# Attention's row sums: eight pair sums of a half folded into one by accumulating DMAs, multiplied with ones two halves later

## The reference, cut to what matters

```
q = (x @ q_w.T).reshape(b, s, 16, 32).transpose(0, 2, 1, 3)
k = x @ k_w.T;  v = x @ v_w.T                       # one head of 32
scores = jnp.einsum('bhqd,bkd->bhqk', q, k) * SCALE
attn = jax.nn.softmax(scores, axis=-1)
out = jnp.einsum('bhqk,bkd->bhqd', attn, v)
```

## Time and profile before

| what | us |
|---|---|
| median of three runs (4967.91 to 4980.27) | 4971.23 |
| profiled execution, its own time | 4975.68 |
| its span | 4974.1 |
| busy in the span: PE / PEld | 4767.6 / 3697.1 |
| busy in the span: DVE / ACT / POOL | 2952.8 / 2256.3 / 2330.5 |

### The profile page before, as it was taken

How to read it: one execution, slowest core, us unless ns; L and a number is a source line. 1 busy time by engine, 2 the same in 40 slices (tenths; PEclk the granted TensorE clock), 3 DMA queues, 4 the chain that set the end, 5 groups by cost and what they waited for, 6 DMA issues and landing times. The chain is left out here.

```text
span 4974.1 us, 92399 instructions
## 1 busy us (share of the span) xinstructions
PE 4767.6 (96%) x32156; PEld 3697.1 (74%) x32157; DVE 2952.8 (59%) x5707; ACT 2256.3 (45%) x4559; POOL 2330.5 (47%) x1775
## 2 busy tenths in 40 slices
PE   6999996999999999999999699999899999999999
PEld 4788884666666666666666478888799987689999
DVE  6222226788888888888883622222655548675444
ACT  4222224366666666666663422222544435454343
POOL 1545424188888888888882154542411107420000
PEclk8999997899999999999999799999999999999999
DMA  7223227544334443343434722322533212251110
GB/s 222 79 88 105 89 76 265 191 81 78 76 76 79 79 80 75 76 80 78 81 67 148 220 82 91 105 86 78 176 102 102 94 62 78 65 195 52 52 52 31
DMA packets 254023, 496.58 MB, mean 100 GB/s; under 512 B 31728, under 2 KB 86000, under 8 KB 253424
## 3 DMA queue, kind: packets, MB, share of 16 engines
q0 software_dynamic: 62656, 220.24, 19.5%
q1 hardware_dynamic: 191024, 271.73, 16.6%
HBM read 262.74 MB, written 121.63 MB: 77 GB/s over the span
## 5 line engine op out<-in xcount | busy, mean ns | idle before, releaser
L1463 DVE TENSOR_REDUCE attend_mx<-attend_am_ps 128x1 f32<-128x512 f32 x2048 | 1247.8, 677 | 197.8 <-PE attend_am_ps L1338 197.7
L1449 POOL TENSOR_TENSOR attend_pairs<-attend_pt 128x1024 f32<-128x1024 f32 x512 | 1219.0, 2421 | 231.8 <-ACT attend_pt L1429 231.5
L1429 ACT ACTIVATE attend_pt<-attend_sc_ps 128x512 f32<-128x512 f32 x2048 | 1053.8, 620 | 307.6 <-PE attend_sc_ps L1326 305.4
L1338 PE MATMUL attend_am_ps<-attention_kst,attend_qst 96*128 96x512 f32 x2048 | 866.0, 427 | 9.0 <-DMA attend_qst<-q_parts 8.9
L1326 PE MATMUL attend_sc_ps<-attend_qst,attention_kst 98*128 98x512 f32 x2048 | 817.2, 400 | 1.3 <-ACT attend_pt L1429 1.1
L1338 PEld LDWEIGHTS attend_am_ps<-attention_kst,attend_qst 96*128 96x128 f32 x2048 | 392.7, 192 | 243.3 <-issue 102.9
L718 DVE TENSOR_TENSOR expert_ac<-expert_gu_ps,expert_gl 128x512 f32<-128x512 f32 x144 | 99.5, 691 | 668.7 <-ACT expert_gl L682 663.8
L1353 PE MATMUL attend_pv_ps<-attend_pt,attention_v 128*32 128x256 f32 x8192 | 491.6, 380 | 0.0
L1326 PEld LDWEIGHTS attend_sc_ps<-attend_qst,attention_kst 98*128 98x128 f32 x2048 | 389.3, 190 | 83.4 <-ACT attend_pt L1429 9.8
L1353 PEld LDWEIGHTS attend_pv_ps<-attend_pt,attention_v 128*32 128x32 f32 x8192 | 259.9, 110 | 188.9 <-issue 23.8
L1817 ACT ACTIVATE ffn_sg<-ffn_gu_ps,ffn_gs 128x256 f32<-128x256 f32 x352 | 166.7, 474 | 508.4 <-PE ffn_gu_ps L1738 508.3
(11 more groups left out here) (348 smaller groups left out, 9310.7 us busy)
## 6 DMA issues: line engine op xcount, KB each, us to landing
attend_pairs<-attend_pairs POOLq DMA_DIRECT2D x192, 512.0 KB
weights_raw<-experts_dram POOLq DMA_DIRECT2D x76, 512.0 KB
ys<-expert_ob SPq DMA_DIRECT2D x144, 256.0 KB
attend_qst<-q_parts SPq DMA_DIRECT2D x192, 128.0 KB, 3.3
yn<-route_yb SPq DMA_DIRECT2D x64, 256.0 KB
ffn_xb<-x SPq DMA_DIRECT2D x64, 256.0 KB, 3.4
ffn_rb<-x SPq DMA_DIRECT2D x64, 256.0 KB
keyvalue_xb<-x SPq DMA_DIRECT2D x64, 256.0 KB, 2.8
```

The lines of the kernel that those rows point to most:

```text
L1338: pe.matmul(am[:, bank, :], qst[0:KROWS, n % 2, h * HALF + hd, :], kst[0:KROWS, o:o + 4 * P], start=True, stop=True).then_inc(am_rdy, 1)
L1429: act.activation(pt[:, u % RING, g * 4 * P:(g + 1) * 4 * P], sc[:, s % SBANKS, :], ACT.Exp, scale=HD ** -0.5).then_inc(p_rdy, 1)
L1449: pool.tensor_tensor(pairs[:, j, :], pt[:, 2 * p % RING, :], pt[:, (2 * p + 1) % RING, :], ALU.add).then_inc(pair_rdy, 1)
L1463: dve.tensor_reduce(mx[:, hh, block:block + 1], am[:, am_slot["max", a] % MBANKS, :], AX.X, ALU.max).then_inc(mx_rdy, 1)
```

## The change

- A half's eight pair sums are folded into one by four DMAs, all accumulating, issued by GpSimd. Fold 0 adds slots of pairs 2, 3 to those of 0, 1 (1 MB, both slots in one DMA), fold 1 adds 4, 5, fold 2 adds 6, 7 (1 MB each), and fold 3 adds the second slot to the first (512 KB). They are issued after GpSimd's pair 4 and 7 of the same half and pair 2 and 5 of the next (FOLD_AFTER = 4, 7, 10, 13), each after a wait for the fold before it.
- TensorE multiplies the one folded slot by ones: one group of four matmuls in a half, at batch 0 two halves later, after a wait for fold 3. The last half isn't folded: its eight pair sums are multiplied one by one at the end.
- The slots of pairs 0 and 1 exist in three sets, the other six once: `pairs` has 12 slots in place of 8. GpSimd's pair 0 of a half waits for the sums three halves back, its pairs 2, 4 and 6 for folds 0, 1 and 2 of the half before.
- The copied values are kept in three sets, the copied sums in two; `keep_sums`, the reciprocals and the output of a half come four batches (one half) later. `raw` (the output weights as loaded) takes the place of the last tiles of `attn`.

```diff
-QUADS = (1, 3, 5)
-LAG_QUAD = 3
-LAG_SUM = 2
+SETS = 3
+FOLD_AFTER = (4, 7, 10, 13)
...
+        def slot(half, j):
+            return 2 * (half % SETS) + j if j < 2 else 2 * SETS + j - 2
...
+            def add_up(half, j, first, last):
                 for i in range(4):
+                    ins = pe.matmul(pv[HD * i:HD * (i + 1), 1, :], const["ones"][:, 0:HD], pairs[:, slot(half, j), 2 * P * i:2 * P * (i + 1)],
+                                    start=first, stop=last, skip_group_check=True)
+                if last:
+                    ins.then_inc(sum_rdy, 1)
+
+            def sums(half):
+                pe.wait_ge(fold_in[-1], 16 * (half + 1))
+                add_up(half, 0, False, True)
...
-                if at == 0 and half:
+                if at == 0 and half >= 1:
                     pe.wait_ge(vals_kept, half)
-                if at == 1 and half:
-                    pe.wait_ge(sums_kept, half)
-                for done, j in batch_sums(c):
-                    sums(done, j)
+                if at == 1 and half >= 2:
+                    pe.wait_ge(sums_kept, half - 1)
+                if at == 0 and half >= 2:
+                    sums(half - 2)
                 for u in range(c * BATCH, (c + 1) * BATCH):
                     values(u)
             pe.wait_ge(vals_kept, HALVES)
-            for done, j in batch_sums(BATCHES):
-                sums(done, j)
+            sums(HALVES - 2)
+            pe.wait_ge(sums_kept, HALVES - 1)
+            for j in range(HPAIRS):
+                pe.wait_ge(pair_rdy, RING // 2 + (HALVES - 1) * HPAIRS + j + 1)
+                add_up(HALVES - 1, j, j == 0, j == HPAIRS - 1)
...
+            def fold(half, k):
+                if not 0 <= half < HALVES - 1:
+                    return
+                to = slot(half, 0)
+                if k:
+                    pool.wait_ge(fold_in[k - 1], 16 * (half + 1))
+                if k < len(FOLD_AFTER) - 1:
+                    pool.wait_ge(pair_rdy, RING // 2 + half * HPAIRS + 2 * k + 4)
+                    put, get = pairs[:, to:to + 2, :], pairs[:, slot(half, 2 * k + 2):slot(half, 2 * k + 2) + 2, :]
+                else:
+                    put, get = pairs[:, to, :], pairs[:, to + 1, :]
+                pool.dma_start(put, get, accum_op=ALU.add).then_inc(fold_in[k], 16)
+
             for p in range(N * PAIRS):
                 half, j = divmod(p, HPAIRS)
-                if half:
-                    pool.wait_ge(sum_rdy, sums_until(half - 1, j))
+                if j == 0 and half >= SETS:
+                    pool.wait_ge(sum_rdy, half - SETS + 1)
+                if j >= 2 and j % 2 == 0 and half:
+                    pool.wait_ge(fold_in[j // 2 - 1], 16 * half)
                 pool.wait_ge(p_rdy, SBANKS + 4 * p + 4)
-                pool.tensor_tensor(pairs[:, j, :], ...).then_inc(pair_rdy, 1)
-                if j in QUADS:
-                    pool.wait_ge(pair_rdy, RING // 2 + p + 1)
-                    pool.dma_start(pairs[:, j - 1, :], pairs[:, j, :], accum_op=ALU.add).then_inc(quad_in[QUADS.index(j)], 16)
+                pool.tensor_tensor(pairs[:, slot(half, j), :], ...).then_inc(pair_rdy, 1)
+                for k, after in enumerate(FOLD_AFTER):
+                    if j == after % HPAIRS:
+                        fold(half - after // HPAIRS, k)
...
-                half, at = divmod(c - PER_HALF - 1, PER_HALF)
+                half, at = divmod(c - 2 * PER_HALF - 1, PER_HALF)
                 if half >= 0:
                     shares(half, at)
                     if at == PIECES - 1:
                         output(half)
```

More of the change, by code:

```diff
@@ L1214, in attention_stage @@
         pt = mem.sb("pt", [P, RING, HALF * P])
-        pairs = mem.sb("pairs", [P, HPAIRS, HALF * P])
+        pairs = mem.sb("pairs", [P, SETS * 2 + HPAIRS - 2, HALF * P])
         mx = mem.sb("mx", [P, HEADS, KBLOCKS])
@@ L1220, in attention_stage @@
         inv = mem.sb("inv", [P, 2 * P])
-        raw = mem.sb("raw", [P, DC, D])
-        kept = mem.sb("kept", [P, 2, 2, 2 * P])
+        vals = mem.sb("vals", [P, SETS, 2 * P])
+        whole = mem.sb("whole", [P, 2, 2 * P])
+        raw = attn[:, NT - DC:NT, :, :].rearrange("p c h q -> p c (h q)")
         sc = mem.ps("sc", [P, SBANKS, 4 * P])
@@ L1227, in attention_stage @@
         m_in = mem.sems("m_in", 2)
-        quad_in = mem.sems("quad_in", len(QUADS))
+        fold_in = mem.sems("fold_in", len(FOLD_AFTER))
         w_in, whi_rdy = mem.sem("w_in"), mem.sem("whi_rdy")
@@ L1240, in attention_stage @@
         PER_HALF = QT // BATCH
-        SUMS = len(QUADS) + HPAIRS - 1 - QUADS[-1]
         AHEAD = 2 * BATCH + SBANKS
@@ L1355, in values @@
                 ins.then_inc(pv_rdy, 1)
-            def sums(half, j):
-                if j in QUADS:
[L1360 to L1364, removed]
-                for i in range(4):
-                    ins = pe.matmul(pv[HD * i:HD * (i + 1), 1, :], const["ones"][:, 0:HD], pairs[:, slot, 2 * P * i:2 * P * (i + 1)],
-                                    start=False, stop=(j == HPAIRS - 1), skip_group_check=True)
-                ins.then_inc(sum_rdy, 1)
+            def add_up(half, j, first, last):
+                for i in range(4):
+                    ins = pe.matmul(pv[HD * i:HD * (i + 1), 1, :], const["ones"][:, 0:HD], pairs[:, slot(half, j), 2 * P * i:2 * P * (i + 1)],
[5 more added lines that the diff above has]
+                add_up(half, 0, False, True)
             for c in range(-LEAD // BATCH, BATCHES):
@@ L1407, in keep_values @@
             def keep_values(half):
-                if half >= 2:
-                    act.wait_ge(o_rdy, half - 1)
+                if half >= SETS:
+                    act.wait_ge(o_rdy, half - SETS + 1)
                 act.wait_ge(pv_rdy, RING + QT * (half + 1))
-                act.activation(kept[:, half % 2, 0, :], pv[:, 0, :], ACT.Copy).then_inc(vals_kept, 1)
+                act.activation(vals[:, half % SETS, :], pv[:, 0, :], ACT.Copy).then_inc(vals_kept, 1)
             def keep_sums(half):
@@ L1417, in keep_sums @@
                     act.wait_ge(inv_rdy, PIECES * (half - 1))
-                act.wait_ge(sum_rdy, SUMS * (half + 1))
-                act.wait_ge(pv_rdy, RING + min(QT * (half + 1) + BATCH, N * UNITS))
-                act.activation(kept[:, half % 2, 1, :], pv[:, 1, :], ACT.Copy).then_inc(sums_kept, 1)
+                act.wait_ge(sum_rdy, half + 1)
+                act.wait_ge(pv_rdy, RING + min(QT * (half + 2) + BATCH, N * UNITS))
+                act.activation(whole[:, half % 2, :], pv[:, 1, :], ACT.Copy).then_inc(sums_kept, 1)
             for s in range(PIECES_ALL):
@@ L1433, in _ @@
                     keep_values(half)
-                if i == 0 and at == 0 and half > 0:
-                    keep_sums(half - 1)
+                if i == 0 and at == 0 and half >= 2:
+                    keep_sums(half - 2)
             keep_values(HALVES - 1)
+            keep_sums(HALVES - 2)
             keep_sums(HALVES - 1)
@@ L1443, in _ @@
                 pool.tensor_tensor(w_lo[:, c, :], raw[:, c, :], w_hi[:, c, :].bitcast(F32), ALU.subtract)
+            def fold(half, k):
[10 more added lines that the diff above has]
+                pool.dma_start(put, get, accum_op=ALU.add).then_inc(fold_in[k], 16)
             for p in range(N * PAIRS):
                 half, j = divmod(p, HPAIRS)
-                if half:
-                    pool.wait_ge(sum_rdy, sums_until(half - 1, j))
+                if j == 0 and half >= SETS:
+                    pool.wait_ge(sum_rdy, half - SETS + 1)
+                if j >= 2 and j % 2 == 0 and half:
+                    pool.wait_ge(fold_in[j // 2 - 1], 16 * half)
                 pool.wait_ge(p_rdy, SBANKS + 4 * p + 4)
-                pool.tensor_tensor(pairs[:, j, :], pt[:, 2 * p % RING, :], pt[:, (2 * p + 1) % RING, :], ALU.add).then_inc(pair_rdy, 1)
-                if j in QUADS:
-                    pool.wait_ge(pair_rdy, RING // 2 + p + 1)
-                    pool.dma_start(pairs[:, j - 1, :], pairs[:, j, :], accum_op=ALU.add).then_inc(quad_in[QUADS.index(j)], 16)
+                pool.tensor_tensor(pairs[:, slot(half, j), :], pt[:, 2 * p % RING, :], pt[:, (2 * p + 1) % RING, :], ALU.add).then_inc(pair_rdy, 1)
+                for k, after in enumerate(FOLD_AFTER):
+                    if j == after % HPAIRS:
+                        fold(half - after // HPAIRS, k)
         @block.vector
@@ L1487, in shares @@
                 cut = slice(2 * P // PIECES * piece, 2 * P // PIECES * (piece + 1))
-                dve.reciprocal(inv[:, cut], kept[:, half % 2, 1, cut]).then_inc(inv_rdy, 1)
+                dve.reciprocal(inv[:, cut], whole[:, half % 2, cut]).then_inc(inv_rdy, 1)
             def output(half):
@@ L1494, in output @@
                 dve.wait_ge(vals_kept, half + 1)
-                dve.tensor_tensor(attn[:, n, h, :], kept[:, h, 0, :], inv[:], ALU.mult).then_inc(o_rdy, 1)
```

(5 more changed lines are left out.)

## The result

The changed kernel takes 5042.1 us (median of four, 5021.6 to 5044.4), the kernel before 4972.5 (four): a ratio of 1.013 (interval 1.010 to 1.016). It is slower by 70 us, where 110 us faster was forecast. The profiled execution took 5021.6 (span 5019.9), 46 over before's. The last copy of sums now starts at 2684.68 against 2642.31, 42 us later, so nearly all of the 46 lies in the attention stage.

The account below looks back on a forecast made before the run. TensorE was taken as the bound; 110 us saved by fewer groups, 0.6 added at the end and all else 0 gave -109 on 4975.7: 4866, or 4862 as a median, range 4848 to 4885 (4848 to 4925 with rivals).

Parts of the forecast that it names:

- Part 2: VectorE in a half: its order isn't moved and its room ahead of each batch suffices; cost 0, upper bound 37 us.
- Part 4: DMA engines and chain of folds: share 0.90 after 0.40, every fold lands in time; no wait, bounds 0 to 31 us.
- What bounds the kernel: Attention stage: TensorE sets the time at 25.86 us a half, VectorE second with 3.06 us of room, GpSimd third with 4.34.
- what a group costs: Sum matmuls on TensorE: a group of four costs 0.42 to 0.45 us, read from batch lengths.
- Part 1: Sum matmuls on TensorE: 249 of 320 groups go, a half falls to 24.11 us, 110 us saved.
- Part 3: GpSimd's queue: a 1 MB issue takes 0.87 us (upper bound 1.73), 22.4 us of work in 24.1; hidden, cost 0.
- rival B: GpSimd becomes the bound: 1 MB issues take 1.73 us, 25.0 us a half, 53 us saved, 4918; chance 0.14.
- The question of the 2048 elements: GpSimd's fold issues: if the accumulating unit's 2048 limit were exclusive, an 8 KB row needs two descriptors, issue nearer 1.73 us.
- rival D: DMA engines become the bound, folds slower per byte than quads; slower than before, about 5120 at 1.33 times; chance 0.09.
- Part 5: Moved waits and the end: waits stay or loosen; one group, a wait for ScalarE's copy, then eight groups; cost 0.6 us.

Follow-up runs that it names:

- f1: The changed kernel with the four folds of a half and every wait for them left out, row sums incomplete: 4866.8 us, ratio 0.979 to before.
- f3: The changed kernel with each fold cut to 128 columns of one slot (64 KB), same places and waits: 4923.6 us, ratio 0.991 to before.
- f4: The kernel before with each quad's DMA issued one pair later, nothing else moved: 5033.9 us, ratio 1.012 to before.
- f2: The changed kernel without the 4 KB transfers of row maxima into the queries' tile after the first four halves, folds whole: 4927.7 us, ratio 0.992.
- g4: The changed kernel without VectorE's subtraction of the split maxima and the first of two reductions, low part set to zero: 4861.5 us, ratio 0.977.
- v1: The changed kernel with maxima computed 28 units ahead in place of 24, split and turn one batch earlier: 4911.2 us, ratio 0.987.
- v2: The changed kernel with folds issued after pairs 3, 7, 9 and 13 in place of 4, 7, 10 and 13: 4958.6 us, ratio 0.997.

## Why the prediction was wrong, step by step

Two steps failed. Part 2 took VectorE's durations as fixed, and Part 4 left the transfers of the maxima out of its deadlines; both terms stood at 0 in the sum.

- **What bounds the kernel, what a group costs**: right. Saved time in f1 is 103 us (4969.9 - 4866.8), forecast 109.
- **Part 1**: right, 568 records; batches 0 and 1 at 6.23 and 5.8.
- **Part 2, VectorE**: the step that failed first. I carried VectorE's durations over unchanged ("its order isn't moved", cost 0). The split in batch 2 has an operation whose end is set by GpSimd's running addition, and Part 3 itself moved that addition by putting an issue between pairs 2 and 3. 0.51 us became 1.37. Worth 57 us here (f3 less f1), 64 in f4. The delay reaches TensorE through the next maximum, whose bank the turn needs. The row was there to be read: a 128x8 subtraction of 0.5 us, three times the 0.18 us of the reductions beside it, ending with the addition.
- **Part 3, GpSimd**: the issue costs 0.92 at the mean, with a median of 0.863, for a forecast of 0.87; rival B, with 1.73, is out. The time is independent of bytes (f3). The question of the 2048 elements, which the prediction left open, has its answer in the packets that the profile counts: 32381 for the 225 folds of the 1500 us below, 144 each, as before (25056 for 174 quads), so a row of 8 KB was not split in two. "Hidden, cost 0" was right for GpSimd's own time and wrong for what its moved additions meet. The queue, and its issues of 1 MB and of 512 KB with the median us to landing, 1000 to 2500:

```profile
q0 software_dynamic: 32381, 206.57, 70.6%
...
attend_pairs<-attend_pairs POOLq DMA_DIRECT2D x169, 1024.0 KB, 7.5
attend_pairs<-attend_pairs POOLq DMA_DIRECT2D x56, 512.0 KB, 8.0
```

- **Part 4, the DMA engines**: the share went from 0.40 to 0.78, the folds' deadlines held (2.9 us of waits). But I set deadlines only for the folds and the query loads, and left out the smallest transfers on the same engines, 4 KB of maxima two at a time, which TensorE wants some 5.3 us after they are sent. Behind fold 0 they took 6.7 (114 us, f2). The result is slower than before, as in rival D (chance 0.09), and by rival D's resource, but not by its mechanism: 1 MB folds took no more engine time a byte than quads (70.6% for 394 times 512 KB in 1500 us, 2.69 each, against 2.87).
- **Part 5**: right.

The two losses are chained: the late subtraction (0.9 us) makes the maxima late by enough to be sent just behind fold 0 and not ahead of it. So 171 us of loss (57 and 114) over f1's 4867 hang on one VectorE operation; g4 shows it. Earlier maxima (v1) and an earlier fold 0 (v2) each take away the wait for the rows while the subtraction stays long (929 and 1526 ns), so the second loss can be had back without the first.

The Trainium skill has the first rule: SBUF — State Buffer, "Who interferes with whom", says that a VectorE instruction with two SBUF inputs contends with a GpSimd instruction that reads SBUF. The traces agree: in every kernel with the subtraction, it ends 0.02 to 0.04 us after an addition of GpSimd in the stretches read, whatever its length, wherever the ends of the additions can be told apart. The Trainium skill has the second too: DMA: Bandwidth & Descriptors, "Queues, rings and completion order", says that a DMA engine takes its queues in turn, but drains a whole packet of some nine to seventeen descriptors from one before it switches. Since a 1 MB fold is eight rows of 8 KB for each engine if its 128 rows are spread evenly over the 16, a small transfer would then stand behind all of it; the 6.7 us here agree, and so does v2, but no run here shows in what portions an engine takes its queues.

## What to carry to other kernels

When an edit gives GpSimd even one more issue between two operations, look for VectorE operations with two operands in SBUF that run beside it, and see whether they end where a GpSimd operation ends; such a meeting is a wait that no list of waits shows. When bulk transfers are added, write down the deadline of every transfer on the engines, the smallest first. And if an expected gain is missing, leave out the added work (f1) and then halve it by kind, bytes against issues (f3): two runs split the loss here.

## What the runs showed of the hardware that I had not expected

- A VectorE subtraction of 128x8 takes 0.43 us in f1 and 1.9 at most in the stretch read of v2, by where GpSimd's addition ends. Even the 0.43 ends with an addition (1503.36 and 1503.39 in the lines of f1 below), so no run here shows what it takes by itself; the reductions of one operand beside it take 0.18 to 0.19.

```profile
1498.64 4.72 POOL L1453 TENSOR_TENSOR attend_pairs<-attend_pt 128x1024 f32<-128x1024 f32 x2 [1.44 <-ACT attend_pt L1417]
```

```profile
1502.96 0.43 DVE L1473 TENSOR_TENSOR attend_msplit<-attend_neg,attend_msplit 128x8 fp32r<-128x8 f32 x1
```

- The product of values and reciprocals (128x256), the other operation with two operands in SBUF that VectorE has in each half, behaves alike. In a gap between additions it took 0.43 us (v1, at 1513.31). In the kernel before, the one after and g4 it took 0.62, 0.63 and 1.13 in the stretches read, and ended each time 0.3 us after an addition did. Its means are 446 ns in v1, 640 in the changed kernel and 903 in g4.
- The issue of an accumulating DMA takes 0.92 us at the mean, with folds of 64 KB as with folds of 1 MB. GpSimd's additions take 2384 ns with no folds (f1), 2453 with folds of 64 KB (f3) and 2455 in the changed kernel, so bytes are not what slows them: an addition right behind an issue is recorded with 2.6 to 2.7 us and starts before the issue's record ends. In g4 they take 2673 and the issues 1114; why is not shown.
- Two transfers of 4 KB, the first sent 0.6 us after the issue of a 1 MB accumulate, were there for TensorE 6.7 us after they were sent. Sent 0.6 us ahead of that issue (g4), they were there by the time they were wanted, about 5.3 us after.
